# Two attention blocks on one core: block 1's value product in three split products over two query tiles, rows scaled ahead of the transposes, three sets of banks in the last round

## The reference, cut to what matters

```python
# block 0: 4 heads of 32 channels
_x = group_norm(x, 32 groups)
q, k, v = lin(_x, Wq, bq), lin(_x, Wk, bk), lin(_x, Wv, bv)
w = softmax(q.k / sqrt(128)) over the 1024 keys, per head
x1 = (x + lin(w.v, Wp, bp)) / sqrt(2)
# block 1: one head of 128 channels
h = group_norm(x1, 8 groups)
q, k, v = split(h @ qkv_w.T + qkv_b)
attn = softmax(q @ k.T / sqrt(128))
out = (attn @ v) @ proj_w.T + proj_b + x1
```

## Time and profile before

| what | value |
|---|---|
| median of 3 runs | 1681.25 us (1680.1 to 1683.15) |
| profiled execution, its own time | 1681.49 us |
| span of the profiled execution | 1679.7 us, 1.8 us less than its time |
| mean granted PE clock | 0.975 of full |
| PE busy | 1604.5 us (96% of the span) |
| DVE busy | 1162.1 us (69%) |
| ACT busy | 1069.1 us (64%) |
| POOL busy | 1130.2 us (67%) |
| one steady round (start of a pv piece to the same one a round later) | 97.0 us |

### The profile page before, as it was taken

How to read it: one execution, slowest core, us unless ns; L and a number is a source line. 1 busy time by engine, 2 the same in 40 slices (tenths; PEclk the granted TensorE clock), 3 DMA queues, 4 the chain that set the end, 5 groups by cost and what they waited for, 6 DMA issues and landing times.

```text
span 1679.7 us, 25530 instructions
## 1 busy us (share of the span) xinstructions
PE 1604.5 (96%) x9319; PEld 1067.4 (64%) x9319; DVE 1162.1 (69%) x1961; ACT 1069.1 (64%) x1825; POOL 1130.2 (67%) x535
## 2 busy tenths in 40 slices
PE   3888899999999999999999999999999999999888
PEld 2343466666666666666667666766666676766567
DVE  3677677777777777777777777677777767775342
ACT  1245576766667666766766676767667676767634
POOL 2088787676668867666786767668776766788700
PEclk8599899999999999999999999999999999999989
DMA  6132304041311404141140414113041412200000
GB/s 201 66 76 72 68 13 131 21 126 39 101 45 57 108 20 126 39 117 36 51 107 21 125 39 126 38 64 83 33 114 38 126 38 66 67 20 8 7 7 20
DMA packets 47660, 111.69 MB, mean 66 GB/s; under 512 B 5808, under 2 KB 6448, under 8 KB 47536
## 3 DMA queue, kind: packets, MB, share of 16 engines
q1 hardware_dynamic: 47536, 110.06, 23.5%
HBM read 67.84 MB, written 41.94 MB: 65 GB/s over the span
## 4 chain that ended last, share of the span: by engine, by line
PE 89%; DVE 5%; ACT 3%; DMA 2%; issue 1%; POOL 0%; SPq 0%; ACTq 0%; POOLq 0%
PE bank L899 15%; PE acc L838 14%; PE scores L877 14%; PE scores L820 14%; PE scores L864 7%; PE scores L856 4%; PE acc L904 3%; PE bank L908 3%; PE scores L857 3%; PE scores L858 3%; PE bank L904 3%; DVE halfmax L707 3%; PE bank L922 2%; PE bank L926 2%; ACT turned L569 1%
## 5 line engine op out<-in xcount | busy, mean ns | idle before, releaser
L510 POOL TENSOR_TENSOR sum<-sum,probs 128x1024 f32<-128x1024 f32 x448 | 1049.7, 2379 | 398.2 <-PE acc L838 397.0
L707 DVE TENSOR_REDUCE halfmax<-bank 128x1 f32<-128x512 f32 x1024 | 678.1, 685 | 246.3 <-PE bank L899 242.4
L549 ACT ACTIVATE probs<-scores 128x512 f32<-128x512 f32 x896 | 516.2, 598 | 185.4 <-PE scores L820 181.9
L899 PE MATMUL bank<-k_stack,q_stack 96*128 96x512 f32 x1024 | 445.4, 455 | 29.0 <-DVE halfmax L707 11.1
L820 PE MATMUL scores<-q_stack,k_stack 97*128 97x512 f32 x1024 | 448.6, 455 | 2.3 <-DMA q_stack<-neg 2.2
L899 PEld LDWEIGHTS bank<-k_stack,q_stack 96*128 96x128 f32 x1024 | 196.4, 194 | 162.0 <-DVE halfmax L707 90.6
L877 PEld LDWEIGHTS scores<-v,turned 128*128 128x128 f32 x1952 | 252.3, 191 | 38.5 <-ACT turned L569 19.2
L877 PE MATMUL scores<-v,turned 128*128 128x128 f32 x1952 | 259.5, 276 | 4.3 <-ACT turned L569 3.8
L820 PEld LDWEIGHTS scores<-q_stack,k_stack 97*128 97x128 f32 x1024 | 194.6, 192 | 99.5 <-issue 78.6
L562 ACT ACTIVATE probs<-scores,negmax 128x1024 f32<-128x1024 f32 x128 | 142.7, 1115 | 155.9 <-DVE negmax L746 155.9
L838 PE MATMUL acc<-probs,v 128*32 128x512 f32 x1792 | 222.5, 608 | 0.0
(11 more groups left out here) (86 smaller groups left out, 1293.9 us busy)
## 6 DMA issues: line engine op xcount, KB each, us to landing
q_stack<-parts_dram SPq DMA_DIRECT2D x96, 256.0 KB, 5.2
k_stack<-parts_dram SPq DMA_DIRECT2D x96, 256.0 KB, 7.2
xin<-x_dram SPq DMA_DIRECT2D x16, 512.0 KB, 3.4
x<-x_dram SPq DMA_DIRECT2D x16, 512.0 KB, 3.5
parts_dram<-q_hi SPq DMA_DIRECT2D x16, 512.0 KB, 2.6
parts_dram<-q_lo SPq DMA_DIRECT2D x16, 512.0 KB, 3.1
parts_dram<-k_hi SPq DMA_DIRECT2D x16, 512.0 KB, 3.1
parts_dram<-k_lo SPq DMA_DIRECT2D x16, 512.0 KB, 4.2
```

What stands on the lines that cost most here:

```text
L510: pool.tensor_tensor(total, total, probs[:, ring_slot(i, half, kt), 2 * two:2 * two + 2, :], ALU.add).then_inc(added[two], 1)
L549: act.activation(dst, score_bank(i, index), ACT.Exp).then_inc(exp_done, 1)
L707: dve.tensor_reduce(halfmax[:, h, t, half:half + 1], banks[p][:, :], AX.X, ALU.max).then_inc(bank_free[p][VE], 1)
L899: mm = pe.matmul(dst[:, :], qs[0:SPLIT, q_half(i, arg // FIRST), h, tile(t % 4)], ks[0:SPLIT, i % 2, h, halves(half)], start=True, stop=True)
```

## The change: what it does

Tiles go in pairs, 16 gaps for each. The exponentials of a tile are multiplied by one over their row sum before they are transposed ("even", on ACT in the rounds, on POOL in the last round). The transposed tile is copied by ACT as a rounded high part (`turned_high`), and DVE subtracts that from the bank for a low part (`turned_low`); both are F32R. The values are split in the same manner (`value1_high`, `value1_low`). A pair's value product has the values as weights and 256 query columns, three F32R products for each of eight key tiles (24 in all), into one of the two shared banks; its result has channels on the partitions, so the transposes back, `mixed1` and `oevict` are gone, and bias and residual are added for 256 columns at a time. The next tile's score1 waits for this tile's `turned_low`.

In the last round three sets of banks rotate over the tiles. POOL leaves out its last four additions of image 15 (`DIRECT = 2`) and sums on PE reads those exponentials itself. Tiles stand 4 gaps apart as before. The maxima and the other pieces have new gaps, and some weights are scaled in place.

```diff
-TILE_GAPS, TILE_FIRST = 8, 41
-            ("max1", t, 0, None, None, first + 1),
-            ("exp1", t, 0, None, first + 1, None),
-            ("rinv", t, 0, None, None, first + 3),
-            ("turn", t, 0, first + 3, first + 3, None),
-            ("pv1a", t, 0, first + 5, first + 6, None),
-            ("pv1b", t, 0, first + 6, None, None)]
+PAIRS, PAIR_GAPS, PAIR_FIRST = KT // 2, 16, 41
+def pair_pieces(p, first):
+    return [("score1", (2 * p, 0), 0, first, None, None),
+            ("score1", (2 * p, 1), 0, first + 1, None, None),
+            ("max1", 2 * p, 0, None, None, first + 1),
+            ("exp1", 2 * p, 0, None, first + 2, None),
+            ("rinv", 2 * p, 0, None, None, first + 2),
+            ("even", 2 * p, 0, None, first + 2, None),
+            ("turn", 2 * p, 0, first + 4, first + 4, first + 6),
+            ("score1", (2 * p + 1, 0), 0, first + 9, None, None),
+            ("score1", (2 * p + 1, 1), 0, first + 9, None, None),
+            ("max1", 2 * p + 1, 0, None, None, first + 9),
+            ("exp1", 2 * p + 1, 0, None, first + 10, None),
+            ("rinv", 2 * p + 1, 0, None, None, first + 10),
+            ("even", 2 * p + 1, 0, None, first + 11, None),
+            ("turn", 2 * p + 1, 0, first + 12, first + 12, first + 13),
+            ("pv1", p, 0, first + 14, None, first + 16),
+            ("pv1b", p, 0, first + 15, None, None)]
...
 MAX_EARLY = (
-    19, 25, 27, 27, 28, 35, 36, 36, 38, 43, 44, 47, 51, 53, 53, 57, 59, 60, 64, 65, 66, 67, 67, 68, 69, 71, 76, 77,
-    78, 81, 82, 83, 86, 87,
+    20, 21, 26, 27, 29, 32, 33, 35, 35, 36, 38, 40, 45, 48, 50, 51, 53, 53, 53, 55, 59, 60, 61, 64, 65, 67, 68, 69,
+    74, 75, 77, 81, 83,
 )
 MAX_LATE = (
-    19, 24, 25, 28, 29, 30, 31, 31, 33, 34, 41, 44, 45, 47, 48, 50, 51, 54, 55, 59, 60, 62, 62, 67, 68, 69, 73, 73,
-    74, 79,
+    25, 26, 27, 28, 29, 30, 35, 36, 42, 44, 46, 50, 51, 53, 55, 57, 57, 58, 61, 66, 67, 68, 72, 73, 74, 75, 75, 77,
+    82, 85, 86,
 )
...
-LAST_TILE, LAST_FIRST, LAST_SPACE = 3, 3, 4
+LAST_TILE, LAST_FIRST, LAST_SPACE, LAST_WAIT = 3, 2, 4, 2
+DIRECT = 2
...
-            ("rinv", t, offset, None, None, first + 2), ("turn", t, offset, first + 5, first + 5, None),
-            ("pv1a", t, offset, first + 10, first + 10, None), ("pv1b", t, offset, first + 10, None, None)]
+            ("rinv", t, offset, None, None, first + 3), ("turn", t, offset, first + 6, first + 6, first + 8)] + (
+                [("pv1", t // 2, offset, first + 11, None, first + 13),
+                 ("pv1b", t // 2, offset, first + 11, None, None)] if t % 2 else [])
...
+    ("save", 1, -1, None, 4, None), ("sums", 1, -1, 4, 4, None), ("recip", (1, 0), -1, None, None, 4),
+    ("recip", (1, 1), -1, None, None, 4), ("recip", (1, 2), -1, None, None, 5), ("recip", (1, 3), -1, None, None, 5),
+    ("proj", 1, -1, 12, None, 12), ("stats1", 1, -1, None, None, 12),
+    ("mean1", 0, -1, 13, None, 13), ("var1", 0, -1, 15, None, 15), ("affine1", 0, -1, None, None, 17),
+    ("norm1", 0, -1, None, 18, None),
+    ("q1", 0, -1, 20, 20, 20), ("q1", 1, -1, 20, 20, 20), ("k1", 0, -1, 20, 20, 21), ("k1", 1, -1, 20, 20, 21),
...
+LAST_POOL = [("scale", 1, -1), ("even", LAST_TILE, -2), ("even", LAST_TILE + 1, -2), ("even", LAST_TILE + 2, -2),
+             ("rstd", 1, -1)] + [("even", t, -2) for t in range(LAST_TILE + 3, KT)] + [("even", t, -1) for t in range(KT)]
...
     def tile_set(j, t):
-        return (t - LAST_TILE) % 2 if KT * j + t >= TWO_SETS else 0
+        return max(KT * j + t - MORE_SETS, 0) % 3
...
+            def even(j, t):
+                act.wait_ge(rinv_done, KT * j + t + 1)
+                act.activation(probs1_of(j, t), probs1_of(j, t), ACT.Identity,
+                               scale=rowinv[:, t:t + 1]).then_inc(evened, 1)
...
+            def turned_high(j, t):
                 act.wait_ge(turned_full, KT * j + t + 1)
...
+                act.copy(turned_of(j, t // 2, 0)[:, :, tile(t % 2)],
+                         score1_pair(j, t).rearrange("p (k n) -> p k n", n=C)).then_inc(turned_hi, 1)
...
+            def turned_low(j, t):
+                dve.wait_ge(turned_hi, KT * j + t + 1)
+                hi, lo = [turned_of(j, t // 2, low)[:, :, tile(t % 2)] for low in range(2)]
+                dve.tensor_tensor(lo, score1_pair(j, t).rearrange("p (k n) -> p k n", n=C), hi.bitcast(F32),
+                                  ALU.subtract).then_inc(turned_lo, 1)
...
+                elif half == 0 and KT * j + t:
+                    pe.wait_ge(turned_lo, tiles_before(j, t))
...
             def turn(j, t):
-                pe.wait_ge(exp1_done, KT * j + t + 1)
+                T = KT * j + t
+                if T < MORE_SETS:
+                    pe.wait_ge(evened, T + 1)
+                else:
+                    pe.wait_ge(evened_late, T + 1 - MORE_SETS)
...
+            def pv1(j, p, part_of):
...
+                    pe.wait_ge(turned_lo, KT * j + 2 * p + 2)
+                hi, lo = [turned_of(j, p, low) for low in range(2)]
                 for kt in range(4 * part_of, 4 * part_of + 4):
-                    mm = pe.matmul(out1(j, t), turned_of(j, t)[:, tile(kt)], v1[:, kt, :], start=kt == 0,
+                    pe.matmul(banks[b][:, 0:2 * C], v1[0][:, kt, :], hi[:, kt, :], start=kt == 0, stop=False)
+                    pe.matmul(banks[b][:, 0:2 * C], v1[0][:, kt, :], lo[:, kt, :], start=False, stop=False)
+                    mm = pe.matmul(banks[b][:, 0:2 * C], v1[1][:, kt, :], hi[:, kt, :], start=False,
                                    stop=kt == KT - 1)
```

More of the change, by code:

```diff
@@ L99 @@
[L99 to L104, removed]
@@ L201, in bank_uses @@
         if piece[0] in BANKED:
-            b = 2 if piece[0] in IN_ACC and piece[1] == 0 else 0 if free[0] <= free[1] else 1
+            own = piece[0] in IN_ACC and piece[1] == 0 and (piece[0][1] == "0" or piece[2] < images - 1)
+            b = 2 if own else 0 if free[0] <= free[1] else 1
             uses[piece] = (b, sum(counts[b]), counts[b][0], counts[b][1], last[b])
@@ L216, in bass_two_attention_blocks @@
     uses = bank_uses(images)
-    TWO_SETS = KT * (images - 2) + LAST_TILE
+    MORE_SETS = KT * (images - 2) + LAST_TILE
+    MORE_PAIRS = MORE_SETS // 2
     def bank_of(piece):
@@ L275, in bass_two_attention_blocks @@
         v0 = sb("v0", [C, 2, KT, C])
-        v1 = sb("v1", [C, KT, C])
+        v1 = [sb(n, [C, KT, C], F32R) for n in ("v1_hi", "v1_lo")]
         probs = sb("probs", [C, RING, HEADS, HALF])
@@ L279, in bass_two_attention_blocks @@
         probs1 = sb("probs1", [C, N])
-        turned = sb("turned", [C, N])
-        mixed1 = sb("mixed1", [C, KT, C])
+        turned = [sb(n, [C, KT, 2 * C], F32R) for n in ("turned_hi", "turned_lo")]
         mix = sb("mix", [C, N])
@@ L439, in store @@
             def store(i, half):
-                piece = ("out", half, i)
-                sp.wait_ge(bank_free[bank_of(piece)][VE], given_back(piece))
+                for p in range(2 * half, 2 * half + 2):
+                    piece = ("pv1", p, i)
+                    sp.wait_ge(bank_free[bank_of(piece)][VE], given_back(piece))
                 sp.dma_start(out_dram[i][:, halves(half)], x1[:, i % 3, halves(half)]).then_inc(stored, 16)
@@ L517, in _ @@
             for i in range(images):
-                for n in range(2 * ADDS):
+                for n in range(2 * ADDS - (2 * DIRECT if i == images - 1 else 0)):
                     half, kt, two = n // ADDS, n // 2 % (KT - 1) + 1, n % 2
@@ L528, in _ @@
                                 rstd(arg, i + offset)
-            scale(1, images - 1)
-            rstd(1, images - 1)
+            for piece, arg, offset in LAST_POOL:
+                if piece == "scale":
+                    scale(arg, images + offset)
+                elif piece == "rstd":
+                    rstd(arg, images + offset)
+                else:
+                    even_late(images + offset, arg)
         @block.scalar
@@ L555, in save, with left_by_block0 @@
                     act.wait_ge(bank_full[bank_of(piece)], filled(piece))
-                act.copy(mix[:, halves(half)], acc[:, :]).then_inc(saved, 1)
+                act.copy(mix[:, halves(half)], acc).then_inc(saved, 1)
+            def left_by_block0():
+                piece = ("sums", 1, images - 1)
+                act.wait_ge(bank_full[bank_of(piece)], filled(piece))
             def exp1(j, t):
                 act.wait_ge(negmax_done, KT * j + t + 1)
-                if KT * j + t:
+                if tiles_before(j, t) is None:
+                    left_by_block0()
+                elif KT * j + t:
                     act.wait_ge(turned_full, tiles_before(j, t))
@@ new lines, in value1_low, with output @@
+            def value1_low(half, i):
+                piece = ("v1", half, i)
+                p = bank_of(piece)
+                dve.wait_ge(v1_hi, 2 * i + half + 1)
+                hi, lo = [v1[low][:, 4 * half:4 * half + 4, :].rearrange("p t n -> p (t n)") for low in range(2)]
```

(18 more changed lines are left out.)

236 lines of the change are left out of this document (115 added, 121 removed).

## The result

The changed kernel takes 1765.04 us (median of 4 runs, 1756.72 to 1765.97), the kernel before 1681.54: 1.0485 times, interval 1.0452 to 1.0518. It is slower, by 83.5 us; 1659 was forecast, and the range ended at 1693. The profiled execution took 1764.62 us with a span of 1762.8. Three of the four runs had a mean granted clock of 0.966 or 0.967; the fourth had 0.975, as the kernel before, and took 1756.72 us, so some 8 of the 83.5 us come and go with the clock.

The account below looks back on a forecast made before the run. PE, 96% busy, was taken to set the round. From 1681.5 us, 11.5 for the steady rounds and 11 for the last round were subtracted, giving 1659 us; the forecast's own range was 1640 to 1678, the wider one 1628 to 1693.

Parts of the forecast that it names:

- the fourth rival: Pair products on PE: weight loads don't overlap, 0.23 us a product, 10.6 us more per image, 1829 us; chance 0.02.
- the step from 93.4 to 96.2 us a round: Steady round: from all new waits covered by old ones, 93.4 us, to the forecast 96.2, 0.8 less than before.
- +3.5 for new waits: Steady round on PE: turns short by 1.6 us and pair products by 1.9, taken in full.
- -2.0 for old ones: Steady round: 2.0 us of PE's old waits, on ACT's copy and DVE's maxima, go.
- +1.3 for DVE's load: Steady round: DVE gets 11.5 us more work, 83.8 us in all, which adds 1.3 us.
- Stay: Round 0 and the start of round 1 have no block 1, so their time was to stay unchanged.
- The new score1 order needs nothing: Block 1: turned_low comes by gap first + 6 and + 13, ahead of the score1 that waits; no cost.
- the first term: Last round, up to image 15's first score1: at about 1619 in place of 1630.95, 12 us earlier.
- the second was to lose: Last round, image 15 from its first score1 to the end: 46 us against 44.5.
- the second was the right side: Rival, steady round: PE waits in full on even and turned_low, DVE delays maxima; 98.6 us, total 1695; chance 0.20.
- the first rival: New waits hidden: rounds of 93.4 us, 14 us off the last round, total 1616; chance 0.24.
- half the new waits: Variant of the hidden-waits rival: with half the new waits in the rounds, total 1630 us.

Follow-up runs that it names:

- 10: Changed kernel, q0's second bank given back one gap later so pair 1 gets another bank, gap 53's maxima spread over 52 to 54: 1786.4 us, 1.063.
- 15: Changed kernel with pair 1's bank change, earlier second-tile scaling for pairs 0 and 2 alone, last round's scaling on ScalarE: 1729.9 us, 1.029.
- 14: Kernel before plus a VectorE reduction of 1024 columns behind each tile's reciprocal, on which nothing waits: 1715.8 us, 1.020.
- 5: Changed kernel with VectorE subtracting only the first key tile, 128 of 1024 columns: 1716.3 us, 1.021.
- 6: Changed kernel with subtraction cut to 128 of 1024 columns, plus a VectorE reduction of 1024 columns on which nothing waits: 1743.5 us, 1.038.
- 13: Kernel before, with GpSimd leaving out its last four additions of image 15 and sums reading those exponentials itself: 1676.1 us, 0.9967.
- 8: Changed kernel with the scaling of the last round's 13 tiles on ScalarE in place of GpSimd: 1744.9 us, 1.038.

## Why the prediction was wrong

**What held.** PE's saving: 0.120 us for a new product, 3.6 us of pieces less a round. The Trainium skill, "TensorE: Matmul & The Clock Gate" (Part 3, The mechanism), states that a weight load overlaps with running products only when the row group differs; the trace disagrees here. Without overlap it would have been the fourth rival's 0.23. The prices of ACT (1.146 against 1.24) and DVE (1.218 against 1.23; 82.3 us of a round against 83.8) held as well, and so did the place of the new waits: turns on even, pair products on turned_low.

**What failed: the step from 93.4 to 96.2 us a round.** It had +3.5 for new waits, -2.0 for old ones that they would cover, +1.3 for DVE's load: 2.8. The measured losses rose by 7.7 (4.0 to 11.7), and the round by 4.1.
- The turns, priced at 1.6 us of waits, lost 3.1 us by gaps (0.34, 0.86, 0.20, 0.19, 1.08 and 0.40 for tiles 4, 5, 6, 0, 1, 2). For a pair's second tile I let one exponential slip between exp1 and even and took 4.5 us from score1 to turn. The trace has exp1 through at 2.7 and even started at 4.0, since that exponential itself waits for PE's next score behind a pv; the turn came at 5.2.
- The pair products lost 5.1 us (1.78 in gaps 7 and 8, 0.85, 0.69, 1.75 for pairs 1, 2, 3, 0) against 1.9. Two things went wrong there. I counted one wait of theirs, DVE's subtraction, and not the other, the bank: pair 1, at nothing in the sum, was the largest, and another bank for it gave back 1.2 us (10, 15). And the subtraction itself was under-priced, 3.3 us for pairs 2, 3 and 0 against 0.5, 0 and 1.4: pair 3's, at nothing in the sum, starts half a microsecond behind the copy, as DVE has a maximum in between. What gap 8 waits for stays open.
- DVE's load costs 2.3 us in the old kernel (14) and 1.15 for the subtraction in the new one (5 against 6), against 1.3 taken. I had called DVE's idle time room. It isn't: it stands where PE has not yet filled a bank for it.
- Of the 2.0 us of old waits at most 0.5 was seen to go: all gaps but those of the turns and pair products lose 3.5 us (11.7 less 3.1 and 5.1), and the whole round lost 4.0 before. The waits for maxima rose from 3.2 to 8.1 us. That DVE catches up while PE waits was argued and not read from a row; PE waiting also means no new maximum for DVE.

**Round 0 and the lists.** "Stay" was wrong: 10.8 us. At the same mean granted clock, 0.90, round 0 takes 85.9 us with the old lists (13) and 90.1 with the new ones (15): the lists cost some 4 us there, and which of them wasn't tried. The rest went with the clock: 0.96 over round 0 in the kernel before, 0.84 in the changed one, and no profiled run with the new lists had over 0.92 there (88.9 us).

**The end: 11 us shorter was forecast behind the last pv, it is 7.7 longer (98.5 against 90.8), and 10.1 us more are lost just before it.** These 10.1 us are round 15's second half, which the sum took for a steady round. Here it is beside the kernel before (columns as above; before is the second line):

```profile
1626.73:1664.35 37.62, 31.33 (x165) 17.95 (x168) 14.35 (x18) 22.98 (x37) 25.76 (x12) 0.82 0.00 0
```

```profile
1561.40:1588.94 27.54, 26.82 (x180) 15.77 (x179) 9.09 (x13) 19.32 (x34) 26.28 (x12) 1.00 0.03 10
```

There are no maxima there, as no next image follows, so PE has little to put between a tile's pieces; it idles for 6.3 us in place of 0.7, and 4.5 us more of busy time come with a granted clock of 0.82 in place of 1.00. "The new score1 order needs nothing" fails here: tile 3's score1 waits for scaling, turn, copy and subtraction in a row, and the last pv stands behind it. The chain of waits from there on, against the earlier trace rows:

```profile
1654.57 1.16 ACT probs L608
1655.77 1.11 PE scores L937 x8
1656.90 1.02 ACT turned_hi L620
1657.95 1.24 DVE turned_lo L808
1659.23 0.50 PE scores L925
...
1661.25 3.10 PE scores L908 x16
1664.35 2.63 PE bank L1006 x24
...
1667.62 3.40 DVE rb L786 x4
1671.09 1.26 POOL mix L523
1672.35 2.84 POOL probs L539
...
1703.88 0.23 PE scores L925
...
1731.53 2.85 POOL probs L539
1734.43 1.09 PE scores L937 x8
...
1744.06 2.85 POOL probs L539
1746.95 1.97 PE scores L937 x8
```

Sums follows the pv at once (1.5 us was forecast) and the reciprocals start 3.3 us behind it (5.0 was). But the scaling by POOL stands in the chain at every second turn, 12.5 us apart where I had 9.5 for a pair, because it takes 2.84 us. I had priced it by POOL's one tensor-scalar of that size in the old trace, 1.13, which has an immediate and a column as operands where the new one has a column alone. 14.3 us of the end are this (8), 11.2 of them behind the last pv. The start of image 15, forecast 30 us behind the last pv, came at 39.5 (1703.88 - 1664.35), before it was 42.0; from there to the end of the span it is 59.0 us in place of 48.8. So the 12 us that the first term was to gain came as 2.5, and the 1.5 us that the second was to lose (46 against 44.5) came as 10.2. The third set of banks shows no gain of its own; it was not tried alone.

Of the rivals, the second was the right side: waits on even and turned_low, and DVE in front of the maxima, at 98.6 us a round. It had 0.20, and its 1695 is still 70 us short: 2.5 us a round, rounds 0 and 14, and the end. In the first rival, "half the new waits" doesn't give 1630: half of 3.5 us a round, 14.4 times, is 25 us over 1616, so 1641. That moves no bound.

**Still open.** Of the 4.1 us of a steady round, the experiments place 1.05 (wait for the subtraction), 1.15 (its load), up to 1.4 (scaling), 1.2 (pair 1's bank); with PE's 3.6 us saved there is 7.7 to explain, so some 2.9 us, among others in gaps 0, 8, 32 and 34, is placed by gap but not by cause. Only the bank's saving and that of an earlier scaling were seen to add (15), so this remainder is rough. The clock has no part in the 4.1: it is full in both rounds. A bank of its own for the pairs' results was not tried.

## What to carry to other kernels

Where an in-order engine is the bound and the order is packed, price a change by what each piece waits for and holds, the bank too: cheaper products saved 3.6 us a round, and the waits around them cost 7.7. An engine that is 75% busy has no room if its idle time falls where it is starved; a load that nothing waits for cost 2.3 us for 8. A price worked out for a steady round doesn't hold where the filling work ends: half a round without maxima lost 10.1 us. Before a saving in the body, look at the chain in the last round: four additions and one gap there gave 8 us, with no risk to the order of the rest.

## What the runs showed of the hardware that wasn't expected

- A GpSimd tensor-scalar of 128x1024 float32 in SBUF takes 2.84 us (2.837 to 2.850, 13 of them) with a column as its one operand, and 1.13 with an immediate multiply and a column add.
- An F32R product of 256 columns with a weight load of its own stands 0.120 us from the next, of 512 columns 0.23; at the lower of the clock's two levels (1.2 GHz) the chain has 0.21 for 256.
- Two executions of the same code in round 0 granted mean clocks of 0.84 and 0.92 and took 93.65 and 88.9 us.
